# The encoder's output gate and halved cell moved from VectorE to ScalarE

## What is computed

```python
def step(carry, xw):
    h, c = carry
    z = xw + h @ U
    i, f, g, o = jnp.split(z, 4, axis=-1)
    i = jax.nn.sigmoid(i)
    f = jax.nn.sigmoid(f)
    g = jnp.tanh(g)
    o = jax.nn.sigmoid(o)
    c = f * c + i * g
    h = o * jnp.tanh(c)
    return ((h, c), h)
...
h_fwd = _lstm(x @ Wf + bf, Uf, reverse=False)
h_bwd = _lstm(x @ Wb + bb, Ub, reverse=True)
```

## Time and profile before

| | us |
|---|---|
| runs of the kernel | 4503.42, 4507.6, 4514.02; median 4507.6 |
| profiled execution | 4507.31 |
| its span, first to last instruction | 4505.5 |
| encoder, first tanh of the fwd cell to last of the bwd cell | 612.44 to 2496.79 |

### The profile page before, as it was taken

One profiled execution on the slowest core, in us unless ns is written; L12 is line 12 of the kernel. 1 busy time (PEld: TensorE's weight loads), 2 busy tenths in 40 slices (PEclk: granted clock), 3 DMA queues, 4 the chain that ended last, 5 costly groups with the idle time before them and its releaser, 6 DMA issues. The chain is left out here.

```text
span 4505.5 us, 136669 instructions
## 1 busy us (share of the span) xinstructions
PE 3622.8 (80%) x46409; PEld 2097.8 (47%) x46409; DVE 3390.7 (75%) x23281; ACT 1759.5 (39%) x9834; POOL 83.9 (2%) x130
## 2 busy tenths in 40 slices
PE   7999978888888888888888588777788777788777
PEld 2222245555555555555555344444444444444443
DVE  5555579999999999999999666666666666666665
ACT  2322334444444444444444233333333333333333
POOL 7000000000000000000000000000000000000000
PEclk8999965555555555555555566666666666666667
DMA  2000000000000000000000000000000000000000
GB/s 74 15 19 14 12 6 3 3 3 3 3 3 3 3 3 3 3 3 3 3 3 3 4 5 6 5 6 6 6 5 6 5 6 6 6 5 6 5 6 6
DMA packets 50001, 32.25 MB, mean 7 GB/s; under 512 B 38173, under 2 KB 47389, under 8 KB 49318
## 3 DMA queue, kind: packets, MB, share of 16 engines
q1 hardware_dynamic: 49318, 23.77, 2.1%
HBM read 15.37 MB, written 8.39 MB: 5 GB/s over the span
## 5 line engine op out<-in xcount | busy, mean ns | idle before, releaser
L721 PE MATMUL bank<-enc_hi,u_lo 128*128 128x16 f16 x8192 | 561.0, 179 | 358.5 <-DVE enc_hi L769 354.8
L721 PE MATMUL bank<-ring_hi,u_lo 128*128 128x16 f16 x4096 | 305.5, 194 | 439.8 <-DVE ring_hi L769 437.6
L721 PEld LDWEIGHTS bank<-enc_hi,u_lo 128*128 128x128 f16 x8192 | 375.0, 107 | 573.5 <-DVE enc_hi L769 457.4
L721 PEld LDWEIGHTS bank<-ring_hi,u_lo 128*128 128x128 f16 x4096 | 189.9, 105 | 915.0 <-DVE ring_hi L769 911.4
L724 PE MATMUL bank<-enc_lo,u_hi 128*128 128x16 f16 x8192 | 563.6, 179 | 5.0
L746 DVE SCALAR_TENSOR_TENSOR planes_dec<-tanh_fi_dec,cell_one_dec 128x32 f32<-128x32 f32 x1024 | 197.8, 193 | 464.2 <-ACT tanh_fi_dec L732 444.5
L721 PE MATMUL bank<-enc_hi,u_hi 128*128 128x16 f16 x8192 | 520.2, 174 | 0.0
L732 ACT ACTIVATE tanh_fi_dec<-bank 128x32 f32<-128x32 f32 x1024 | 202.5, 198 | 807.8 <-PE bank L724 807.8
L739 ACT ACTIVATE tanh_cell_fwd<-scanned_fwd 128x16 f32<-128x16 f32 x1024 | 221.3, 216 | 517.5 <-DVE scanned_fwd L754 517.5
L739 ACT ACTIVATE tanh_cell_bwd<-scanned_bwd 128x16 f32<-128x16 f32 x1025 | 221.5, 216 | 516.7 <-DVE scanned_bwd L754 516.7
L739 ACT ACTIVATE tanh_cell_dec<-scanned_dec 128x16 f32<-128x16 f32 x1024 | 221.1, 216 | 439.2 <-DVE scanned_dec L754 439.2
(11 more groups left out here) (273 smaller groups left out, 8219.6 us busy)
## 6 DMA issues: line engine op xcount, KB each, us to landing
g_rows<-tok_d_gamma_batched_dram SPq DMA_DIRECT2D x8, 512.0 KB, 7.0
x_rows<-in_x_dram SPq DMA_DIRECT2D x16, 256.0 KB, 2.9
kept_h<-tok_ln_h SPq DMA_DIRECT2D x32, 128.0 KB, 2.1
res<-kept_h SPq DMA_DIRECT2D x32, 128.0 KB, 2.5
out_dram<-sums SPq DMA_DIRECT2D x32, 128.0 KB, 2.3
raw_wd<-in_L_attn_Wd_dram SPq DMA_DIRECT2D x2, 256.0 KB
raw_experts<-in_L_ffn_W_dram SPq DMA_DIRECT2D x2, 256.0 KB
raw_u<-in_L_attn_Uf_dram SPq DMA_DIRECT2D x1, 256.0 KB
```

Source lines behind the costliest of these rows:

```text
L721: nc.tensor.matmul(z[g], w[:, g, :], h_hi, start=False, stop=False, skip_group_check=True)
```

## The change

`out_gate` and the halved cell of the encoder are computed by ACT in place of DVE. DVE no longer waits for their semaphores: it waits for `tanh_cell` and `tanh_fi`, which ACT issues behind them. The decoder keeps `dve_rest`.

```diff
+def act_out_gate(nc, act, c, n, half_scale):
+    act.wait_ge(c.s_t_go, n + 1)
+    nc.scalar.activation(c.out_gate[:], c.planes[:, 2, :, 0], ACT.Identity, scale=0.5 * X_SCALE, bias=half_scale
+                         ).then_inc(c.s_out_gate, 1)
+
+
+def act_half_cell(nc, act, c, scans):
+    act.wait_ge(c.s_scan, scans)
+    nc.scalar.activation(c.cell_one[:, 0, :], c.scanned[:, :, 1], ACT.Copy, scale=0.5).then_inc(c.s_cell, 1)
+
+
-def dve_terms(nc, dve, c, n):
+def dve_terms(nc, dve, c, n, own_cell=True):
 
     dve.wait_ge(c.s_t_fi, n + 1)
-    dve.wait_ge(c.s_cell, n + 1)
+    if own_cell:
+        dve.wait_ge(c.s_cell, n + 1)
...
             def _(act):
                 nc.scalar.activation(hello[:], m.ident[:, 0:1], ACT.Gelu)
+                act.wait_ge(s_half_scale, 1)
...
                         act_cell(nc, act, ch[1], n)
+                        if n > 0:
+                            act_half_cell(nc, act, ch[1], n + 1)
                         act_gates(nc, act, ch[0], n, *at(0, step))
+                        act_out_gate(nc, act, ch[0], n, half_scale[:])
                         act_cell(nc, act, ch[0], n)
+                        act_half_cell(nc, act, ch[0], n + 1)
                         act_gates(nc, act, ch[1], n, *at(1, step))
+                        act_out_gate(nc, act, ch[1], n, half_scale[:])
...
                 def hidden(late, n):
                     dve.wait_ge(ch[late].s_tanh_cell, n + 1)
-                    dve.wait_ge(ch[late].s_out_gate, n + 1)
                     dve_hidden(nc, dve, ch[late], n, h[late][0][:])
...
                             hidden(late, n)
-                            dve_terms(nc, dve, ch[d], n)
+                            dve_terms(nc, dve, ch[d], n, own_cell=False)
                             dve_hidden_low(nc, dve, ch[late], n, h[late][0][:], h[late][1][:])
                             dve_scan(nc, dve, ch[d], n)
-                            dve_rest(nc, dve, ch[d], n + 1 + d)
```

More of the change, by code:

```diff
@@ L788, in encoder @@
         hello = sb("encoder_hello", [P, 1], F32)
+        half_scale = sb("encoder_half_scale", [P, 1], F32)
+        s_half_scale = sem("half_scale_set")
         h = list(zip(m.enc_hi, m.enc_lo))
@@ L846, in _ @@
                 own = Links(dve, s_set)
+                nc.vector.memset(half_scale[:], 0.5 * X_SCALE).then_inc(s_half_scale, 1)
                 for d in range(2):
                     ch[d].start(nc, own)
-                nc.vector.memset(ch[1].out_gate[:], 0.0).then_inc(ch[1].s_out_gate, 1)
+                own.link(nc.vector.memset(ch[1].out_gate[:], 0.0))
                 nc.vector.memset(h[0][0][:], 0.0).then_inc(ch[0].s_hi, 1)
```

## The result

The changed kernel takes 4516.95 us (median of 20 runs, 4512.54 to 4522.3), the kernel before 4506.62 us (20 runs, 4498.66 to 4514.02) in the same comparison. The ratio is 1.0026, 95% interval 1.0019 to 1.0033: slower by some 12 us by the ratio (10.3 between the two medians), where 4533 us had been forecast. The direction is right; the size is less than half of the forecast's +26 us.

A forecast was written before the change was run, and what follows sets the result against it. The encoder was taken as bound by a 905 ns dependency ring through ACT and DVE each half-step, not by DVE's busy time. The sum was 4507 + 33 (longer ring) - 7 (long half-steps) = 4533 us, range 4508 to 4578.

The forecast's parts named there:

- Ring: Encoder's chain per half-step, `tanh_cell` back to `tanh_cell`: with the halved cell ahead of `tanh_fi`, 921 ns against 905, +33 us.
- PE's results: Inputs of `tanh_fi`: in hand when ACT is free at 0.13 us, then needed only at 0.226 us; PE gains slack.
- Output gate hidden: On ACT behind the second gate tanh: about 306 ns long, hidden with 0.18 us of cover before `tanh_cell` is due.
- Removed DVE work and waits at 0: Encoder's DVE: two instructions per half-step lying in the wait for `tanh_cell`, and two second waits, each gain 0 us.
- Long half-steps: Encoder's 32 us of DVE issue stalls: fall 40% with DVE's instructions and extra waits, -13 us; with ACT's +6, -7 us.
- ACT's own: Issue stalls of ACT, now in the encoder's ring, might begin to show: 0 to +16 us, +6 taken.
- Marks: Expected encoder timeline signs: `tanh_fi` 0.23 us behind `tanh_cell`, terms following it, DVE idle put down to `tanh_fi`, half-step 0.92 us.

The follow-up runs named there:

- e2: Only the halved cell moved to ACT, the output gate left on DVE, against the kernel before: 4524.9 us, ratio 1.0043.
- h1: The changed kernel with the halved cell moved behind both gate tanhs on ACT: 4471.0 us, 0.9921 of the kernel before.
- f3: The kernel before with two spare ACT instructions between `tanh_cell` and `tanh_fi`: 4742.6 us, one run.
- e1: Only the output gate moved to ACT, the halved cell left on DVE, against the kernel before: 4478.5 us, ratio 0.9939.
- e3: The changed kernel with its two dropped DVE waits put back: 4521.2 us, 1.0042 of the kernel before.
- g3: The changed kernel with one one-column memset ahead of DVE's encoder loop: 4534.0 us, 1.0067 of the kernel before.
- g1: The kernel with only the output gate on ACT, plus two one-column memsets ahead of DVE's encoder loop: 4515.2 us, 1.0024 of the kernel before.
- g4: The kernel before with one one-column memset ahead of DVE's encoder loop: 4506.4 us, ratio 1.0006.
- f1: The kernel with only the output gate on ACT, plus one spare DVE instruction behind the halved cell: 4495.1 us, one run.
- f2: The kernel with only the output gate on ACT, plus two spare DVE instructions behind the halved cell: 4490.8 us, one run.
- f4: The changed kernel with four spare DVE instructions behind the scan, no wait put back: 4523.7 us, one run.

## Why the prediction was wrong in size

**Ring: right.** The forecast was 921 ns against 905; measured 925. Its parts: halved cell 106 ns start to start where 104 was foreseen, `tanh_fi` 178, terms 194; the rest of the 4 ns is in the handovers, 33 to 34 ns each. One reading was off without harm: PE's results were not in hand before the change. `tanh_fi` started 129 ns behind `tanh_cell`, where ready work (the halved cell in the changed kernel) starts at 122, and 22 ns after PE had counted up the semaphore that it waits for; in the changed kernel PE is 142 ns ahead of it. In the stage this is +41 us where +33 stood. e2 shows that it is the halved cell, h1 that it is its place in the queue ahead of `tanh_fi`, and f3 that the sum by ring holds at another length.

**Output gate hidden: right.** 309 ns long (306 foreseen); e1 has 905 ns with it.

**Removed DVE work and waits at 0: right for the ring.** e3 for the waits. For the instructions h1 shows it, whose ring, without either of them, is 904.

**Long half-steps: the step that failed.** The forecast read "they fall by 40%, -13 us", "ACT's own may begin to show", and took -7 us. Measured: -31, to none at all, and none on ACT, in 80 blocks of 128 (5 x 2048 entries). The stalls were taken as something in proportion to the number of entries. They come at a fixed entry of every 128, and cost up to 0.33 us where the stopped instruction is needed at once and nothing where it has to wait anyway. The changed kernel's 6 entries put it on three places. One, `enc_hi`, waits for `tanh_cell` anyway; at the other two, the terms and the wait ahead of the scan, no surplus is seen in any block, so nothing is lost there either. g3, one entry later, pays 9.9 us, and g1 shows the full price. With the forecast's own ring of +33, -31 would have given 4509; with the ring as measured the sum is 4507 + 41 - 31 = 4517 us, the result. That this meets the result to the microsecond is partly luck: the rest of the span moved by +3.5 us, which no term has.

**Why most places show nothing.** The traces also have the start of each instruction packet on q14. Where the 128th entry shows a stop, a packet starts 0.66 to 0.68 us after that entry (medians by place: all five places of the kernel before and of g4, the scan of g1 and g3). Where it shows none, the packet starts sooner: in the changed kernel 0.50 us after `enc_hi`, 0.40 after the terms and 0.35 after the wait ahead of the scan, in h1 0.42 after the terms, in g3 0.45 after `h`, in e1 0.57 and in f1 and f2 0.59 to 0.64 after `enc_hi` or `h`. The reading, argued from these times alone, is that DVE fetches the next block at these places too, but its sequencer reached the entry earlier, by what is missing to 0.67 us, than the entry was carried out, so that the stop was over or nearly over by then.

**Marks.** Of the forecast's marks all but one were met. `tanh_fi` at 0.23 us with 178 ns, the terms 0.03 us behind its end, the half-step of 0.925 us and DVE's fallen share (1315.6 of 1893.5 us, 69%, after 91%) are there, and no long half-step stands in front of ACT's instructions. The idle time of DVE is not put down to `tanh_fi`: `h` was still under way when the terms began to wait, so the view shows 0.0 idle there. A wait shorter than the instruction ahead leaves no idle time to read.

**What a page says.** The Trainium skill, "Runtime: NRT & Kernel Launch", section "Instruction fetch mechanics", has the sequencer stream its program in blocks of 16 KiB, 256 instructions, with the cost of a boundary mostly hidden. The runs differ in the size: the packets on q14 are 8192 bytes for 128 entries. On ACT they agree that the cost is hidden; on DVE they do not: in g1 each boundary costs 0.33 us, 42 us in all.

**Open.** What lets DVE's issue get ahead at a place in one kernel and not in another (`enc_hi` 240 ns before and nothing in f2, `h` 185 in g4 and nothing in g3, terms 257 in f1 and nothing in h1). The kernels in which these are missing have fewer second waits, or in f2 a different one. The skill's "Perfetto Trace Analysis", section "DVE / Act Engine Instruction (TENSOR_ADD, Activation, etc)", has instructions wait in a queue while the sequencer goes on to the next, which would let it get ahead of a stop; the packet times above agree with that. That a second wait holds it up is argued and not shown: e3 puts back only such waits, and f4 has ten entries with one of them, and both fit, but in both the waits also change which instruction the 128th entry is. Nor do the runs show why the stop has the length that it has. Open is also the rest of the span, which lay between 2615 and 2632 us in the profiled executions of these kernels with the same code in it; single executions can't say how much of this is the place of the decoder's program.

## What to carry to other kernels

Find the ring first: an instruction that starts in an engine's idle time costs nothing where it is, and moving it can only cost, unless it lands in idle time again; the changed kernel and h1 differ by 46 us with the same work on each engine, 42.6 of them in the encoder. In an unrolled loop of sub-microsecond instructions, compare two versions by their undisturbed step and their long steps apart, since the second part changes with any instruction added ahead: one or two memsets moved the encoder by -9 to +40 us. Before a gain or a loss under 1% is put down to an edit, move the program by an entry or two and look again: e1's gain holds only where its entries happen to lie (4478.5 us, and 4515.2 two entries later).

## What was not expected of the hardware

- DVE's issue can stop at every 128th entry, second waits counted, for up to 0.33 us (g1: 128 stops, 42.2 us); ACT's never showed, in 48 blocks before the change and 80 after it.
- A second wait takes an entry of DVE's program: 4096 more of them are 32 instruction packets more (e3).
- `tanh_fi` is recorded 178 ns long where it doesn't have to wait for its input, and 198 where it does. That is no general rule of 20 ns for ACT: the halved cell, which never waits, is recorded 200 ns long behind `tanh_cell` in the changed kernel and 218 behind the second gate tanh in h1.
